# The five middle rounds of a gated mixture-of-experts kernel: a loop on the engines' registers, or written out

## The reference

```python
x = x + conv_gate(layernorm_over_channels(x))        # x*sigmoid(conv3x3([max_c, mean_c]) + b)
t = tokens(x)                                        # one token per pixel, 64 channels
n = layernorm_over_channels(t)
probs = softmax(n @ router_w + router_b)             # 8 experts
top_p, top_i = top_k(probs, 2); top_p /= sum(top_p)
out = t + sum_k top_p[k] * (n @ expert_w[top_i[k]] + expert_b[top_i[k]])
```

## Time and profile before

| | us |
|---|---|
| runs shown, median of 3 | 1703.19 |
| lowest, highest | 1702.29, 1706.99 |
| profiled execution, its own time | 1706.22 |
| its span in the profile | 1704.4 |
| mean granted TensorE clock | 0.94 of full |

### The profile page before, as it was taken

How to read it: one execution, slowest core, us unless ns; L and a number is a source line. 1 busy time by engine, 2 the same in 40 slices (tenths; PEclk the granted TensorE clock), 3 DMA queues, 4 the chain that set the end, 5 groups by cost and what they waited for, 6 DMA issues and landing times.

```text
span 1704.4 us, 37629 instructions
## 1 busy us (share of the span) xinstructions
PE 1460.7 (86%) x12198; PEld 685.1 (40%) x12198; DVE 1345.4 (79%) x1575; ACT 1060.3 (62%) x4015; POOL 1142.8 (67%) x743
## 2 busy tenths in 40 slices
PE   6865899869997799977999779988799788989999
PEld 5763344434443344433444334433344333323333
DVE  3796888788887788878887788868888778977776
ACT  2566677747776577756777558775678624434442
POOL 6335667848676576855768566775667758788775
PEclk9956899989999999999999899999999989999999
DMA  5441465536555455544655445553555444555554
GB/s 173 120 136 39 120 185 173 174 109 184 176 162 154 141 163 172 164 154 127 183 178 168 126 142 173 175 184 121 151 175 154 129 128 136 171 144 172 174 174 127
DMA packets 85883, 260.40 MB, mean 153 GB/s; under 512 B 13744, under 2 KB 13744, under 8 KB 85680
## 3 DMA queue, kind: packets, MB, share of 16 engines
q1 hardware_dynamic: 85680, 257.85, 50.6%
HBM read 206.41 MB, written 51.38 MB: 151 GB/s over the span
## 4 chain that ended last, share of the span: by engine, by line
PE 54%; DVE 18%; issue 9%; ACT 9%; POOL 1%; DVEq 1%; ACTq 0%; POOLq 0%
PE moe L517 31%; PE gb L462 8%; DVE gx L662 8%; PE tm L440 6%; PE moe L511 4%; ACT s L931 3%; DVE u L704 2%; ACT sq L896 2%; PE tm L501 2%; PE tm L455 2%; DVE quarter_key L771 2%; DVE p L701 2%; DVE u L706 1%; PE tm L541 1%; ACT ge L982 1%
## 5 line engine op out<-in xcount | busy, mean ns | idle before, releaser
L662 DVE TENSOR_TENSOR gx<-gb,xd 128x896 f32<-128x896 f32 x672 | 710.5, 1085 | 205.1 <-PE gb L462 192.2
L517 PE MATMUL moe<-gx,wc 128*64 128x448 f32 x3584 | 841.7, 570 | 1.2 <-POOL parts L1119 1.1
L1105 POOL TENSOR_TENSOR gx<-gs,xd 128x896 f32<-128x896 f32 x224 | 519.0, 2317 | 452.3 <-ACT gs L939 423.6
L939 ACT ACTIVATE gs<-gb 128x896 f32<-128x896 f32 x224 | 204.9, 915 | 302.3 <-PE gb L462 301.7
L462 PE MATMUL gb<-s,cg 54*128 54x448 bf16 x1792 | 273.2, 365 | 118.6 <-DVE gx L662 104.9
L896 ACT ACTIVATE sq<-xct 112x64 f32<-112x64 f32 x1400 | 337.8, 243 | 24.6 <-DVE early_s L649 6.4
L517 PEld LDWEIGHTS moe<-gx,wc 128*64 128x64 f32 x3584 | 221.3, 139 | 247.3 <-issue 190.4
L896 ACT ACTIVATION_READ_ACCUMULATOR sq<-xct 112x1 f32 x1400 | 263.1, 188 | 0.0
L1130 POOL TENSOR_TENSOR tt<-xc,a1s 128x896 f32<-128x896 f32 x112 | 235.2, 2100 | 18.7 <-ACT a1s L946 16.0
L440 PE MATMUL tm<-rhs,xa 64*112 64x74 f32 x2800 | 176.7, 267 | 69.4 <-ACT s L931 63.1
L462 PEld LDWEIGHTS gb<-s,cg 54*128 54x128 bf16 x1792 | 61.1, 95 | 398.9 <-DVE gx L662 229.6
(11 more groups left out here) (97 smaller groups left out, 1342.5 us busy)
## 6 DMA issues: line engine op xcount, KB each, us to landing
xd<-in_x_dram SPq DMA_DIRECT2D x448, 224.0 KB, 3.9
xa<-in_x_dram SPq DMA_DIRECT2D x112, 448.0 KB, 4.2
xc<-in_x_dram SPq DMA_DIRECT2D x112, 448.0 KB, 4.4
out_dram<-ot SPq DMA_DIRECT2D x112, 448.0 KB, 3.0
gx<-in_const_g_dram SPq DMA_DIRECT2D x1, 384.0 KB, 4.7
cf<-in_const_f_dram SPq DMA_DIRECT2D x1, 332.5 KB, 2.7
gx<-in_L_ffn_expert_w_dram SPq DMA_DIRECT2D x1, 128.0 KB, 4.5
cf<-in_L_ffn_expert_b_dram SPq DMA_DIRECT2D x6, 2.0 KB
```

What stands on the lines that cost most here:

```text
L517: last = pe.matmul(moe[b * CH:(b + 1) * CH, c, 0:HALF], wc[:, k * CH:(k + 1) * CH], gx[:, u, b, :], start=False, stop=(k == KT - 1), skip_ ...
L662: dve.tensor_tensor(gx[:, i, :, :], gb[:, 2 * slot:2 * slot + 2, 0:HALF], xd[:, v % 2, :, c * HALF:(c + 1) * HALF], ALU.mult).then_inc(sca ...
L939: act.activation(gs[:, j, :, :], gb[:, 2:4, 0:HALF], ACT.Copy).then_inc(gate_out, 1)
L1105: pool.tensor_tensor(gx[:, ND + j, :, :], gs[:, j, :, :], xd[:, v % 2, :, j * HALF:(j + 1) * HALF], ALU.mult).then_inc(scaled_p, 1)
```

## The change

On each of the five engines the loop over rounds 3 to 7 becomes a loop of the program that writes the kernel. The body is then written out five times with `r` as a number:

```diff
             body(2, True, True)
-            with pe.Fori(3, PAIRS) as r:
+            for r in range(3, PAIRS):
                 body(r, True, True)
             body(PAIRS, False, True)
```

More of the change, by code:

```diff
@@ L405, in _ @@
             body(2, True)
-            with sp.Fori(3, PAIRS) as r:
+            for r in range(3, PAIRS):
                 body(r, True)
@@ L852, in _ @@
             body(2, True, True)
-            with dve.Fori(3, PAIRS) as r:
+            for r in range(3, PAIRS):
                 body(r, True, True)
@@ L1052, in _ @@
             body(2, True, True)
-            with act.Fori(3, PAIRS) as r:
+            for r in range(3, PAIRS):
                 body(r, True, True)
@@ L1253, in _ @@
             body(2, True)
-            with pool.Fori(3, PAIRS) as r:
+            for r in range(3, PAIRS):
                 body(r, True)
```

## The result

The changed kernel takes 1681.2 us, the median of 4 runs (1679.26 to 1684.27), against 1704.6 us for the kernel before, now also over 4 runs. The ratio is 0.9864, with a 95% interval of 0.9842 to 0.9887: it is 1.4% faster. The forecast was 1685 us, between 1676 and 1695 us. The profiled execution took 1680.16 us, with a span of 1677.4 us. The two profiled executions differ by 26.1 us, the two spans by 27.0 us. The second figure is what the trace has to account for.

What follows compares the result with a forecast made beforehand. TensorE was taken as busiest, waiting for data and, at taken loop branches, for instruction fetches. Gains of 14.3 + 1.5 + 2.5 = 18.3 us gave 1687.9 us profiled, 1685 us as median, with a range of 1676 to 1695 us.

Steps and rivals of the forecast that it cites:

- weak end: Smallest gain allowed: 10.2 us for the branches, none for registers, two more low-clock hits (+3.0): 7.2 us, or 1696 us.
- four taken branches: Jumps back to the loop's start after rounds 3 to 6: 3.6 us each by difference of passes, -14.3 us in all.
- low clock in mid round: TensorE's lowered granted clock at steps 7 or 12, rounds 3 to 7: four places hit instead of five, -1.5 us.
- register instructions otherwise: Loop register instructions ahead of waits within a pass: between 0 and 5.6 us saved by removing them, middle taken, -2.5 us.
- lower bound: Least price of a taken branch, from TensorE's two bare pauses at a round's start: 2.55 us, 10.2 us for four.
- it depends on where the pause falls in time, not on the loop: Claim on TensorE's pause before L440: round 2 has the same 1.30 us pause without low clock; each hit costs about 1.5 us.
- the low clock falls otherwise: Rival, chance 0.12: none of ten mid-round places is hit, or nearly all; 1679 us, or a small gain with 1694 us.
- the forecast's own case: Main case, chance 0.70: branch, clock and register gains together, 18.3 us, with four of ten places hit by low clock.
- A loss is excluded here, since fewer instructions are issued in the same order.: Premise on removing register instructions within a pass: it could not slow the kernel; the gain lies between 0 and 5.6 us.
- No change: Rival, chance 0.05: the branch is cheap and later passes are longer for another, lasting reason; only 2.5 us go, 1701 us.
- the stall turns into another wait: Rival, chance 0.10: only TensorE's first pause of 1.62 us per branch goes, the rest is stage B's wait; 1694 us.
- The stream runs dry: Rival, chance 0.03: written-out instructions arrive late and engines stall 3.6 us each time; two per round give 1721 us.

Runs made afterwards that it cites:

- r1: Kernel before, with the loop on each engine split into five one-pass loops, so registers stay in rounds 3 to 6 but no branch is taken: 1686.6 us.
- r3: Kernel before, with only TensorE's rounds written out and the other four engines still in the loop: 1714.3 us.
- r7: Kernel before, with all engines' rounds written out except ScalarE's, which keeps its loop: 1707.2 us.
- r5: Kernel before, with VectorE's and ScalarE's rounds written out and TensorE, GpSimd and SyncE still in the loop: 1689.6 us.
- r6: Kernel before, with only ScalarE's rounds written out and the other four engines still in the loop: 1691.6 us.
- r8: Kernel before, with TensorE's, VectorE's and ScalarE's rounds written out and GpSimd and SyncE still in the loop: 1676.3 us.
- r11: Kernel before, with round 7 written out on every engine and the loop kept over rounds 3 to 6: 1695.2 us.
- r2: Kernel before, loop kept on all engines, with a branch prefetch hint at the top of each pass: 1694.2 us.

## Why the prediction was right, and where its terms were off

The time and its sign were right: 1681.2 us within 1676 to 1695 us. (The weak end was worked out as 1696 us.) The terms, set against what the runs and the two traces show:

| term | forecast us | shown us |
|---|---|---|
| four taken branches | -14.3 | about -13.8 (the remainder) |
| low clock in mid round | -1.5 | -7.5 |
| register instructions otherwise | -2.5 | about -0.6 |
| round 8 | not in the sum | -5.2 |
| sum, profiled execution | -18.3 | -27.1 |

**The branches.** The difference of passes was the right price. Of the 21.9 us between the marks, 5 x 1.5 = 7.5 us belong to the low clock and about 0.6 us to the registers, which leaves 13.8 us, 3.5 us for a branch. The passes of r1 give 3.4 us without this subtraction. That it is a fetch was shown by the hint (3711 to 443 ns). The lower bound, TensorE's bare pauses of 2.55 us, was indeed too low. The prediction did not say how the three engines' stalls lie over each other. It is this that makes a part of the change worse than none: in r3 and r7 ScalarE stalls while TensorE does not, and both are slower than the kernel before. In r5 and r6, where ScalarE is freed and TensorE stalls, both are faster.

**The low clock.** Here a step failed. The prediction held that "it depends on where the pause falls in time, not on the loop", and counted hits as chance. The pause was not the same. The loop has 1.30 us there, and the prediction took round 2 to have it too. TensorE's row of the kernel before, in step 12 of round 2, says 1.22 us:

```profile
305.63 1.01 PE L440 MATMUL tm<-rhs,xa 64*112 64x74 f32 x16 [1.22 <-ACT s L931]
```

r1, r5, r6, r7 and the changed kernel show that ScalarE's registers decide whether the pause is 1.30 or 1.22 us. The half of the sentence on time is not refuted: of the places with 1.30 us the clock fell at 29 of 66. The same 0.08 us stood in the earlier trace rows, where it was priced as a delay alone.

What came true was therefore a rival, "the low clock falls otherwise", which had 0.12 and 1679 us with no place hit; the forecast's own case had four. That the time lay in the range is partly luck: the clock gave 6 us more than its term and round 8 another 5 us, and the traced 27.1 us off the 1703.2 us of the forecast would be 1676.1 us, at its very edge. Between the medians the gain was smaller, 23.4 us.

**The registers.** I took the middle between 0 and 5.6 us. The rest that is not the low clock is what r1's rounds show: 201.3 us with registers against 199.7 us in the changed kernel, less the 1.5 us of the clock, 0.1 us a round. Against r1's own round 7, which has no registers and took 199.2 us, it is 0.6 us a round, or 3 us in all. So this term is known only as lying between 0.5 and 3 us, and the remainder for the branches moves with it.

A premise failed here: "A loss is excluded here, since fewer instructions are issued in the same order." Steps 5 and 6 got slower by the change, 12.90 and 13.51 us in round 3 against 12.63 and 13.34 us before, and most other steps got faster by 0.07 to 0.18 us. In the kernel before, GpSimd's registers had made it come second, as in r8 (start us, us):

```profile
411.64 1.08 DVE L686 TENSOR_TENSOR ge<-lg,top 112x896 bf16<-112x896 f32 x1
...
411.67 2.99 POOL L1105 TENSOR_TENSOR gx<-gs,xd 128x896 f32<-128x896 f32 x1 [0.39 <-ACT gs L939]
```

The change took this order away, and VectorE's operation went to 2.98 us. So the near zero of the earlier trace rows is a sum of delays and of this gain, as round 2 has the late VectorE too.

**Round 8** was in no case of the prediction. The argument stopped at the last line of the edit. The 5.2 us rest on one trace on each side, and their cause is open (r11).

**The rivals.** "No change" and "the stall turns into another wait" are out by r1 and r2. "The stream runs dry" is out, as no pause for issue at L462 is left among TensorE's waits. The second rule of the Trainium skill ("Advanced Engine Details and Errata", "Control Flow Timing", about 108 ns for a compare and branch) fits the branch that is not taken (83 ns): by it the gain would have been 0.4 us. TensorE's rows of 3711 ns with a late target and 443 ns with a hinted one decide against it as a price of a taken branch in a body this long.

## What to carry to other kernels

Price a loop by the difference between its first pass, entered by falling through, and the later ones: the branch's own row shows the stall on one engine only, and on others it stands between the branch and the next instruction. Where the loop must stay, hint its branch. When several engines stall together, free first the one that the others wait for: freeing ScalarE alone gave 11 us here, about half of it through the clock, and freeing TensorE alone lost 11 us. Taking instructions out ahead of a wait can cost time as well, because it changes which of two engines comes first. Look for places where two engines want the same port within 0.1 us, and delay the one that nobody waits for.

## What the runs showed of the hardware

- With a pause of 1.30 us in mid round TensorE's granted clock fell to its lower level at 29 of 66 places, at 1.5 us a time. With 1.22 us it fell at none of 90.
- VectorE and GpSimd blocked each other for a whole operation in the pairs shown: 0.05 us of lead on one side made VectorE's 1.08 us operation last 2.98 us. Three waits that are always met, ahead of each GpSimd product, turned this pair round. The kernel became 8 us faster, of which 2.1 us are shown to come from this place.
- A branch row can be short while the engine stalls. VectorE's branch took 63 ns and its next instruction came 3.7 us later.
